# Gated-linear stages of a four-layer network: the spread product at 128 rows, and the shared expert as a ninth weight of one sum

## What is computed

```python
logits = x_flat @ gate_w.T                       # 8 experts
scores = softmax(logits)
w = scores * in_topk                             # 2 of 8 are kept
gu = einsum('nh,eih->nei', x_flat, experts_gate_up)     # 176 hidden rows for each expert
h = silu(g) * u
out = einsum('neh,ne->nh', einsum('nei,ehi->neh', h, experts_down), w)
shared = (silu(x_flat @ shared_gate_w.T) * (x_flat @ shared_up_w.T)) @ shared_down_w.T   # 352 rows
out = out + sigmoid(x_flat @ shared_expert_gate_w.T) * shared
```

## Time and profile before

| | us |
|---|---|
| median of three runs | 2145.08 |
| lowest and highest | 2135.38, 2160.7 |
| the profiled execution | 2133.16, its span 2131.4 |
| fourth phase, from 875 to 1236 in the span | 361 |
| sixth phase, from 1781 to 2124 in the span | 343 |

### The profile page before, as it was taken

How to read it: one execution, slowest core, us unless ns; L and a number is a source line. 1 busy time by engine, 2 the same in 40 slices (tenths; PEclk the granted TensorE clock), 3 DMA queues, 4 the chain that set the end, 5 groups by cost and what they waited for, 6 DMA issues and landing times.

```text
span 2131.4 us, 36931 instructions
## 1 busy us (share of the span) xinstructions
PE 1835.1 (86%) x10156; PEld 1309.6 (61%) x10157; DVE 1246.7 (58%) x3919; ACT 699.0 (33%) x1295; POOL 584.8 (27%) x946
## 2 busy tenths in 40 slices
PE   3759994999643899299999969999999997999998
PEld 2548991555442799177777745555555554777776
DVE  3546884555545588466666554665665553565653
ACT  1115551222110555122322214444444442232231
POOL 2643765555267367512211010000000000000000
PEclk9659996898855899699999969999999999999999
DMA  5111212000011121200000000000000000000001
GB/s 198 40 45 51 59 50 84 23 20 20 0 37 52 51 61 48 61 11 14 16 10 10 1 1 1 1 0 0 0 0 0 0 1 1 1 0 0 0 1 40
DMA packets 61816, 53.69 MB, mean 25 GB/s; under 512 B 8596, under 2 KB 55061, under 8 KB 61350
## 3 DMA queue, kind: packets, MB, share of 16 engines
q1 hardware_dynamic: 52102, 33.83, 5.2%
q0 software_dynamic: 8192, 16.79, 2.7%
q10 hardware_dynamic: 1440, 2.10, 0.3%
HBM read 31.19 MB, written 21.50 MB: 25 GB/s over the span
## 4 chain that ended last, share of the span: by engine, by line
PE 70%; POOL 9%; DVE 8%; issue 7%; DMA 2%; SPq 1%; ACT 1%; POOLq 1%; DVEq 1%; ACTq 0%
PE bk L1021 11%; PE bk L1717 10%; PE bk L582 6%; PE bk L988 5%; PE bk L990 5%; PE bk L989 5%; POOL xs L368 4%; PE bk L999 4%; PE bk L1705 3%; PE bk L575 3%; PE bk L1692 2%; PE bk L1643 2%; PE bk L564 2%; PE bk L566 2%; PE bk L565 2%
## 5 line engine op out<-in xcount | busy, mean ns | idle before, releaser
L112 POOL TENSOR_TENSOR sb_ln_ve<-sb_ln_mv,sb_eps 128x2 f32<-128x2 f32 (+1 forms) x48 | 9.4, 195 | 1024.4 <-DVE sb_ln_mv L104 1024.4
L1077 ACT ACTIVATE sb_sb_<-bk 128x512 f32<-128x512 f32 x224 | 133.8, 598 | 431.2 <-PE bk L990 429.6
L1971 DVE TENSOR_REDUCE sb_sc<-bk 128x2 f32<-128x512 f32 x256 | 164.6, 687 | 159.0 <-PE bk L1692 154.8
L1021 PE MATMUL bk<-sb_wd,sb_sc 128*128 128x128 f32 (+1 forms) x1792 | 254.4, 286 | 0.0
L1021 PEld LDWEIGHTS bk<-sb_wd,sb_sc 128*128 128x128 f32 (+1 forms) x1792 | 221.2, 192 | 46.4 <-issue 42.1
L1717 PE MATMUL bk<-sb_sa,sb_sb_ 128*32 128x256 f32 x1024 | 249.0, 387 | 0.7 <-ACT sb_sc L1866 0.7
L1135 DVE TENSOR_TENSOR sb_sb_<-sb_sb_,bk 128x512 f32<-128x512 f32 x176 | 121.0, 688 | 185.1 <-PE bk L999 184.8
L1879 ACT ACTIVATE sb_sa<-bk 128x512 f32<-128x512 f32 x256 | 151.1, 597 | 185.9 <-PE bk L1705 185.8
L1138 DVE TENSOR_TENSOR sb_sc<-sb_sb_,bk 128x512 f32<-128x512 f32 x224 | 153.8, 687 | 52.9 <-PE bk L990 46.8
L582 PE MATMUL bk<-sb_w2c,sb_sb_ 128*128 x1152 | 152.2, 275 | 0.0
L368 POOL DMA_INDIRECT xs<-sb_xn,sb_send_row x128 | 128.7, 1006 | 79.2 <-DVE sb_send_row L357 42.9
(11 more groups left out here) (294 smaller groups left out, 3618.5 us busy)
## 6 DMA issues: line engine op xcount, KB each, us to landing
sb_sc<-xs SPq DMA_DIRECT2D x144, 64.0 KB, 1.9
ys<-sb_sc SPq DMA_DIRECT2D x36, 256.0 KB, 2.3
xs<-sb_xn,sb_send_row POOLq DMA_INDIRECT x128, 2.2
out<-sb_X SPq DMA_DIRECT2D x1, 2048.0 KB, 8.7
sb_sa<-w SPq DMA_DIRECT2D x1, 1792.0 KB, 14.1
sb_sc<-w SPq DMA_DIRECT2D x1, 1792.0 KB, 17.7
sb_sa<-w_gu SPq DMA_DIRECT2D x1, 1760.0 KB, 6.8
xs<-sb_zeros SPq DMA_DIRECT2D x24, 64.0 KB, 1.6
```

Of the source, the lines that this page charges most:

```text
L1021: ins = pe.matmul(bank[:, j * P:(j + 1) * P], p.hT[0:m, c % HRING, j * P:(j + 1) * P], p.wd[0:m, c * D:(c + 1) * D], start=(c in (0, NRC) ...
L1077: act.activation(p.sg[0:m, c % 2, :], p.bk[c % 2][0:m, :], ACT.Silu).then_inc(p.silu_d.sem, 1)
L1971: dve.tensor_reduce(p.at_m[:, t, :].rearrange("p (q r) -> p q r", r=HQ)[:, q:q + 2, pair % HQ], p.bk[SEARCH_BANKS[f % 3]][:].rearrange("p ...
```

## The change

1. The spread's operands get 128 rows. `gw`, the weights before the transposes, is now a half of the buffer `xn`, 128 columns for each tile, cleared once by POOL in the fourth phase (`gw_zero`); the transposes give 128 rows, `wT` has 128 rows, and the table `w_e` is 128 x 1760 instead of 16 x 1408.
2. The sigmoid is a ninth weight. All 14 chunks get a spread and a multiplication by it, and all sum in bank 4, with one addition at the end. Bank 5 and the four operations of L1154 are gone.
3. That one addition stands behind the first two chunks of the next group, where L1154 stood; L1145 stood ahead of them.

```diff
-NRC = E * I1 // P
-assert NRC * P == E * I1
+NRC = NCH
...
-    pe.matmul(p.bk[7][:], p.sel_e[:, c * P:(c + 1) * P], p.wT[:], start=True, stop=True).then_inc(p.spread.sem, 1)
+    pe.matmul(p.bk[7][0:rows_of(c).stop - c * P, :], p.sel_e[:, rows_of(c)], p.wT[:], start=True, stop=True).then_inc(p.spread.sem, 1)
...
-        ins = pe.transpose(p.bk[6][0:2 * E, j * P:(j + 1) * P], f32(p.gw[:, j, :]), p.ident)
+        ins = pe.transpose(p.bk[6][:, j * P:(j + 1) * P], f32(p.gw[:, j, :]), p.ident)
...
-    routed = c < NRC
-    bank = p.bk[4 if routed else 5]
+    bank = p.bk[4]
     if c == 0:
         pe.wait_ge(p.r_add.sem, p.r_add.at(g))
-    if c == NRC:
-        pe.wait_ge(p.sh_add.sem, p.sh_add.at(TG * g))
...
-    if c < NRC:
-        sw_spread_pe(pe, p, g, c)
+    sw_spread_pe(pe, p, g, c)
...
-    act.activation(p.wT[:], p.bk[6][0:2 * E, :], ACT.Copy).then_inc(p.wt_d.sem, 1)
+    act.activation(p.wT[:], p.bk[6][:], ACT.Copy).then_inc(p.wt_d.sem, 1)
...
-def sw_add_shared(dve, p, g, par):
-
-    dve.wait_ge(p.sh_d.sem, p.sh_d.at(g + 1))
-    dve.wait_ge(p.r_add.sem, p.r_add.at(g + 1))
-    for j in range(TG):
-        x = p.X[:, g * TG + j, :]
-        dve.scalar_tensor_tensor(out=x, in0=p.bk[5][:, j * P:(j + 1) * P], scalar=p.gate1[:, par, j, E:E1], in1=x,
-                                 op0=ALU.mult, op1=ALU.add).then_inc(p.sh_add.sem, 1)
...
-    dve.tensor_copy(p.gw[:, :, 0:E], p.gate1[:, par, :, 0:E]).then_inc(p.gw_d.sem, 1)
+    dve.tensor_copy(p.gw[:, :, 0:E1], p.gate1[:, par]).then_inc(p.gw_d.sem, 1)
...
-    sw_add_routed(dve, p, g)
     if not last:
         for c in range(2):
             sw_product(dve, p, g + 1, c)
-    sw_add_shared(dve, p, g, par)
+    sw_add(dve, p, g)
...
+                    if phase not in p.phases[:n]:
+                        pool.memset(p.xn[:, 1], 0.0).then_inc(p.gw_zero.sem, 1)
...
-    spread = (np.arange(NRC * P)[None] // I1 == np.arange(2 * E)[:, None] % E).astype(np.float32)
+    spread = np.zeros((P, ROWS), np.float32)
+    spread[0:2 * E1] = np.minimum(np.arange(ROWS) // I1, E) == np.arange(2 * E1)[:, None] % E1
```

More of the change, by code:

```diff
@@ L1013, in sw_down @@
     pe.wait_ge(p.hid_d.sem, p.hid_d.at(n + 1))
-    routed = c < NRC
-    bank = p.bk[4 if routed else 5]
+    bank = p.bk[4]
     if c == 0:
         pe.wait_ge(p.r_add.sem, p.r_add.at(g))
-    if c == NRC:
-        pe.wait_ge(p.sh_add.sem, p.sh_add.at(TG * g))
     for j in range(TG):
         ins = pe.matmul(bank[:, j * P:(j + 1) * P], p.hT[0:m, c % HRING, j * P:(j + 1) * P],
-                        p.wd[0:m, c * D:(c + 1) * D], start=(c in (0, NRC) and j == 0),
-                        stop=(c in (NRC - 1, NCH - 1)), skip_group_check=True)
-    if c == NRC - 1:
+                        p.wd[0:m, c * D:(c + 1) * D], start=(c == 0 and j == 0),
+                        stop=(c == NCH - 1), skip_group_check=True)
+    if c == NCH - 1:
         ins.then_inc(p.r_d.sem, 1)
-    if c == NCH - 1:
-        ins.then_inc(p.sh_d.sem, 1)
 def sw_x_pe(pe, p, g):
@@ L1131, in sw_product, with sw_add @@
     dve.wait_ge(p.silu_d.sem, p.silu_d.at(n + 1))
[L1132 to L1136, removed]
+    dve.wait_ge(p.spread.sem, p.spread.at(n + 1))
+    dve.tensor_tensor(sg, sg, p.bk[7][0:m, :], ALU.mult).then_inc(p.mul_d.sem, 1)
+    dve.wait_ge(p.mul_d.sem, p.mul_d.at(n + 1))
     dve.wait_ge(p.up_rows.sem, p.up_rows.at(n + 1))
     dve.tensor_tensor(p.hT[0:m, c % HRING, :], sg, p.bk[2 + c % 2][0:m, :], ALU.mult).then_inc(p.hid_d.sem, 1)
-def sw_add_routed(dve, p, g):
+def sw_add(dve, p, g):
     dve.wait_ge(p.r_d.sem, p.r_d.at(g + 1))
@@ L1163, in sw_gates_dve @@
     dve.wait_ge(p.rt3.sem, p.rt3.at(2 * g + 2))
+    dve.wait_ge(p.gw_zero.sem, p.gw_zero.at(1))
     dve.wait_ge(p.gwt.sem, p.gwt.at(g))
-    dve.tensor_copy(p.gw[:, :, 0:E], p.gate1[:, par, :, 0:E]).then_inc(p.gw_d.sem, 1)
+    dve.tensor_copy(p.gw[:, :, 0:E1], p.gate1[:, par]).then_inc(p.gw_d.sem, 1)
     dve.wait_ge(p.gw_d.sem, p.gw_d.at(2 * g + 1))
-    dve.tensor_tensor(p.gw[:, :, E:2 * E], p.gate1[:, par, :, 0:E], f32(p.gw[:, :, 0:E]), ALU.subtract)\
+    dve.tensor_tensor(p.gw[:, :, E1:2 * E1], p.gate1[:, par], f32(p.gw[:, :, 0:E1]), ALU.subtract)\
        .then_inc(p.gw_d.sem, 1)
@@ L2105 @@
     "swiglu": dict(_PREP, **_COMB, gt_rows=NCH * NG, up_rows=NCH * NG, silu_d=NCH * NG, hid_d=NCH * NG, rtg=NG, rt3=2 * NG,
-                   r_d=NG, r_add=NG, sh_d=NG, sh_add=TG * NG, spread=NRC * NG, mul_d=NRC * NG, gw_d=2 * NG, gwt=NG, wt_d=NG),
+                   r_d=NG, r_add=NG, spread=NRC * NG, mul_d=NRC * NG, gw_d=2 * NG, gwt=NG, wt_d=NG),
 }
@@ L2112 @@
 ONCE = ["const", "tail0", "wrouter", "wts", "wcopy", "wlast", "wshift", "wpe", "wsw", "gab", "gaw", "gar", "atw", "phase_end", "stored",
-        "pe_passed", "dve_passed", "pool_passed", "sel_r"]
+        "pe_passed", "dve_passed", "pool_passed", "sel_r", "gw_zero"]
 NW = 2 * NQ + 2 * H
@@ L2155 @@
     "wgh": ([P, ROWS], F32R), "wgl": ([P, ROWS], F32R), "wuh": ([P, ROWS], F32R), "wul": ([P, ROWS], F32R),
[L2156 removed]
+    "wd": ([P, DOWN], F32), "wT": ([P, W], F32R), "wr1_f": ([P, NL], F32), "wr1h": ([P, NL], F32R), "wr1l": ([P, NL], F32R),
     "ga_w": ([P, NW], F32), "ga_last": ([P, NW], F32), "ga_ln_w": ([P, 2], F32), "ga_ln_b": ([P, P], F32),
@@ L2181, in work_space @@
     w.update(sw_taken=(at.take(P, W), at.take(P, W)))
-    w.update(sel_e=t.w1l[0:2 * E, 0:NRC * P], sel_raw=t.sa[0:2 * E, 0:NRC * P])
+    w.update(sel_e=t.w1l[:, 0:ROWS], sel_raw=t.sa[:, 0:ROWS], gw=t.xn[:, 1].bitcast(F32R))
     w.update(hT=Space(t.sc).take(P, HRING, W), sg=Space(t.sb_).take(P, 2, W))
```

## The result

| | us |
|---|---|
| before, median of 4 runs | 2140.23 (2134.9 to 2160.7) |
| changed kernel, median of 4 runs | 2077.26 (2074.71 to 2095.17) |
| ratio | 0.9707, 95% interval 0.962 to 0.9793 |
| profiled execution before, and its span | 2133.16, 2131.4 |
| profiled execution after, and its span | 2075.43, 2073.7 |

The changed kernel is faster by 3%: 63 us between the medians, 57.7 between the two profiled executions, where 53.3 was forecast. These are the windows of the changed kernel (length; then busy of PE, PEld, DVE, ACT and POOL; then the clock): six groups of the fourth phase and six groups of the sixth.

The account below looks back on a forecast made before the run. PE was taken to bound the kernel at 41.03 us a group. Spreads -57.6, waits +4.2, phase ends -0.9 and fourth phase's start +1.0 sum to -53.3: from 2140.2 to 2087 us, range 2070 to 2112.

Parts of the forecast that it names:

- PE sets the length, and the gap is the spread's row count: Gated-linear groups: PE sets 41.03 us; padding cuts each of eleven spreads from 0.62 to 0.23 us, 4.29 a group.
- The place rival: Spread's bank, wait or step to fp32 makes the gap; padded spreads still cost 0.62 us, 2174 median; 4 in 100.
- the rule weighed there: Spread on PE: one product takes as long with 32 rows as with 128, so padding would bring nothing.
- The 0.49 us: Length of the 16-row spread L999 against 0.40 for L990, read as the trace disagreeing with the skill's rule.
- Three more spreads at 0.23 us: Chunks 11 to 13 of each group get a spread, adding 0.69 us a group on PE.
- Waits for DVE, 0.3 us a group: PE waits at chunk 12's spread and next group's chunk 0 down product: 0.3 us in 14 groups, +4.2.
- The addition: Behind the next group's chunk 1, it makes PE's down product of chunk 0 a few hundredths to 0.1 us late.
- The DVE rival: DVE's bunched gates, norm and combination make PE wait 2 us a group: 2104 as profiled, 2111 median; 7 in 100.
- The end of a phase: The additions on the path there take 0.68 us instead of 1.12, twice: -0.9 us.
- The start of the fourth phase, +1.0 us: Bigger table `w_e` lands 3.1 us later, just inside the gather wait; POOL's clearing adds 0.45; bounds 0.45 and 4.
- The step to the median: Profiled execution before, 2133.16, was fastest of four with middle 2140.2; so 2079.9 as profiled becomes 2087 as median.

Follow-up runs that it names:

- `pad_only`: Kernel before with only the spread's operands padded to 128 rows, shared expert as it was: 2064.66 us, ratio 0.9657; again on chip C 2076.53 us.
- the four row counts: Changed kernel with the spread's product using only 18, 64, 65 or 96 of the 128 rows: 2166.27, 2160.69, 2099.79 and 2077.91 us.
- `two_banks`: Changed kernel with spreads alternating between banks 7 and 5, each waiting for the multiplication two chunks earlier: 2086.01 us, ratio 0.9755; again on chip C 2089.28 us.
- `after_again`: Changed kernel with nothing edited, run once more on another chip, C: 2095.93 us, ratio 0.9803 to the kernel before.
- `pad_table`: `pad_only` with the table `w_e` loaded ahead of the attention's constants: 2077.6 us, ratio 0.9713, on chip B; again on chip C 2077.54 us.

## Why the prediction was right, step by step

- **PE sets the length, and the gap is the spread's row count.** Held, and shown by `pad_only` and the four row counts: 0.39 us for each spread, 4.29 a group. The place rival is out. So is what was drawn from the rule weighed there, that a product of 32 rows takes as long as one of 128 (the Trainium skill, "TensorE: Matmul & The Clock Gate", "Why this matters for your kernels"): here 18 and 64 rows cost the stream 0.39 us more than 128. The 0.49 us that the prediction read as the product's own length was no sign against it, for the padded spread that came late, at 976.18 above, shows 0.50 with 128 rows.
- **Three more spreads at 0.23 us.** Held: `two_banks` without the wait is at 37.45 us a group in the sixth phase, by my count 37.43, and chunks 11 and 13 went from 2.28 to 2.51 us.
- **Waits for DVE, 0.3 us a group.** Half of that. In the loop's groups chunk 12's spread is late by 0.12 to 0.24 us (0.2 forecast), behind the loop not at all, as its load shows, with DVE's end of chunk 11's multiplication ahead of it. The addition was forecast to make chunk 0's down product up to 0.1 late; that product and the chunk behind it keep their pitch. Its timing is read from these rows of DVE, of which the first two are the 6.31 us between chunk 9's and chunk 11's multiplications (6.30 forecast), and the last is the addition:

```profile
969.12 0.69 DVE L1126 TENSOR_TENSOR sb_sb_<-sb_sb_,bk 128x512 f32<-128x512 f32 x1 [2.45 <-PE bk L998]
...
975.43 0.69 DVE L1126 TENSOR_TENSOR sb_sb_<-sb_sb_,bk 128x512 f32<-128x512 f32 x1
...
986.09 0.68 DVE L1136 TENSOR_TENSOR sb_X<-sb_X,bk 128x512 f32 x1
```

- **The DVE rival.** It was right about the place and not about the size in the profiled execution. `after_again` is its case, though from another cause than the one I gave: ACT is late, DVE's bunch behind chunks 9 and 10 then has no room, and a looped group of the fourth phase takes 2.9 us more. PE's waits for DVE are 11.3 us in five groups there, 2.3 each, where the prediction called itself wrong from 1 us a group on: on chip C that step fails, and the first profile doesn't show it. The time, 2095.93, is inside the range, 15 us below the rival's.
- **The end of a phase.** Held: behind PE's last products stands one addition of 0.69 us where L1154's four took 1.12; L1145 stood ahead of their end and was hidden.
- **The start of the fourth phase, +1.0 us: wrong, it cost nothing here.** From the phase's first load (877.61, before 875.23) to the combination it is 13.20 us, before 13.29. The rows of the changed kernel on POOL and DVE:

```profile
877.69 0.52 POOL L2282 MEMSET sb_xn<- 128x512 f32 x1 [5.42 <-POOLq L63]
```

```profile
889.65 1.08 DVE L2324 CAST sb_w1l<-sb_sa 128x1760 fp32r<-128x1760 f32 x1 [16.12 <-DMA sb_sa<-w_e]
890.81 2.31 DVE L478 SCALAR_TENSOR_TENSOR sb_X<-sb_sb_,sb_weight,sb_X 128x128 f32<-128x128 f32 x8
```

  The clearing is on the path as forecast (0.45 counted, 0.52 long), but one of the eight gathers of the kernel before had an issue of 1.38 us instead of 0.94, and of the changed kernel's none had. The two cancel. The long one:

```profile
884.29 1.38 POOL L455 DMA_INDIRECT sb_sb_<-ys,sb_take_row  x1 [0.30 <-issue]
```

  It is the gather beside which DVE cast the table (883.97 to 884.85). In four of the fourteen traces a gather's issue lies beside the cast by more than a few hundredths, and these four alone have a long one at the start of the phase: 1.12 us in `pad_only`, 1.38 before, 1.56 and 1.62 in the two runs of `pad_table`. In the changed kernel the bigger table lands later and its cast begins behind the last gather's issue. So the 0.44 us came off with the change itself; the prediction had no term for it, and that the two are of one size is luck. The table did what was forecast: it landed 8.0 us behind its issue (4.7 + 3.1 counted), and its cast ended at 890.73 (888.2, and 2.4 for the later begin), just as the combination could begin.

**The sum.** Between the two profiled executions, by windows and starts: two sets of six groups, -20.7 each; the last groups' 13 chunks 36.55 to 32.72, -3.8 each; the first groups, -7.4 in the fourth and -0.1 in the sixth phase. These are -56.5 where the prediction had -53.4. The first groups are not the change's doing alone: PE had another clock there. Windows of the kernel before, at the start of the fourth and of the sixth phase, and then of the changed kernel (the clock is the third last number, 0.50 being 1.2 GHz and 1.00 being 2.4):

```profile
910.00:915.00 5.00, 5.00 (x15) 3.56 (x15) 3.11 (x7) 0.60 (x1) 0.00 (x0) 0.50 0.00 0
...
1795.00:1835.00 40.00, 39.33 (x214) 29.81 (x215) 23.56 (x64) 12.33 (x21) 1.21 (x2) 1.00 0.00 1
```

```profile
907.00:912.00 5.00, 4.31 (x23) 3.42 (x22) 2.96 (x5) 1.79 (x3) 0.00 (x0) 1.00 0.05 15
...
1762.00:1803.00 41.00, 40.20 (x223) 34.37 (x224) 25.04 (x68) 13.06 (x21) 1.21 (x2) 0.91 0.00 1
```

Beside a steady group's -3.44, the first group of the fourth phase got 3.9 us more, and that of the sixth 3.4 less, and each time the kernel that falls short is the one whose clock was down for a part of it (at 0.91 for 41 us that is 3.7 us). The phases whose code is unchanged gave +2.4 (the first three) and -3.3 (the fifth). The remainder, -0.3, is the ends of phases: -0.9 for the additions, and twice the 0.23 of chunk 13's own spread. So the change itself gave about 16 x 3.44 = 55 us.

**The step to the median.** I set the forecast at 2087 because the profiled execution before was the fastest of four. The changed kernel's profiled execution lay 1.8 below its own median, not 7 below. Of the 9.7 us by which the result is under the forecast, these are 5.2, the waits at half their size 2, the start of the fourth phase 1, and the rest lies in the clock and in the phases whose code is unchanged. The range holds it.

## What to carry to other kernels

In a stream of full matrix products, a product with 64 rows or fewer cost 0.62 us instead of 0.23 here, since neither its load nor the next one overlapped; if the trace shows "issue" ahead of both loads, fill the rows with zeros to more than 64. Then count what else rides along: each extra product is paid in full, and folding a small part into a padded product is worth it only if it removes more from the bounding engine than it adds. When the bounding engine gets faster, the engines that feed it lose their room, so run the winner on a second chip before its time is believed.

## What the runs showed of the hardware that I had not expected

- The step lies between 64 and 65 rows: 43.0 us a group on the one side, 37.6 to 37.75 on the other, and flat to both sides of it.
- The same program had two times, 2077 and 2096 us, by job or chip, without a difference in the clock of the stretch: ACT resumed about 3 us late in each group beside which POOL issued gathers, 2.57 to 2.73 us behind the start of the last of them. The kernel before, with 0.39 us more room in every chunk with a spread, kept its time on all three chips.
- An indirect transfer takes longer to issue when DVE casts the fp32 table into fp32r beside it: 1.12 to 1.62 us instead of 0.94 in the four traces where they meet, and never in the ten where they don't.
